# Decay attention: the future cleared by a GpSimd select, the value products and their chain one slot later, six weight buffers

## The reference

```python
Q, K, V = proj(Wq, bq), proj(Wk, bk), proj(Wv, bv)      # 16 heads of 8
scores = einsum('bhid,bhjd->bhij', Q, K) / sqrt(8)
delta = ti[:, None] - ti[None, :]                       # query minus key position
scores = where(delta < 0, -inf, scores) + where(delta < 0, 0, -abs(delta))
out = einsum('bhij,bhjd->bhid', softmax(scores), V) @ Wo.T + bo
```

## Time and profile before

| | |
|---|---|
| median of 3 runs | 1361.05 us (1360.64 to 1365.32) |
| profiled execution | span 1358.3 us; its own device time is not listed, so what lies around the span is taken from the median: 2.7 us |
| instructions | 25046 |
| busy share of the span | PE 79%, DVE 65%, ACT 50%, POOL 41%, PEld 52% |
| second pass of the decay attention | first product at 737.7 us, last at 900.2 us |
| PE, 820 to 860 us | 37.82 of 40 us busy, TensorE's granted clock 1.00 |

### The profile page before, as it was taken

One profiled execution on the slowest core, in us unless ns is written; L12 is line 12 of the kernel. 1 busy time (PEld: TensorE's weight loads), 2 busy tenths in 40 slices (PEclk: granted clock), 3 DMA queues, 4 the chain that ended last, 5 costly groups with the idle time before them and its releaser, 6 DMA issues. The chain is left out here.

```text
span 1358.3 us, 25046 instructions
## 1 busy us (share of the span) xinstructions
PE 1079.5 (79%) x8292; PEld 708.4 (52%) x8292; DVE 881.0 (65%) x2989; ACT 685.8 (50%) x1268; POOL 559.6 (41%) x740
## 2 busy tenths in 40 slices
PE   8877777778189553299936999969977999899998
PEld 3222232336188553299934777744434777654544
DVE  6799999976455456377549888843648878840201
ACT  4786656644044301133206888737856888541221
POOL 4489988853633314544426444100025555100000
PEclk9799999998599765599978999989997999999999
DMA  2997000002422206211120000020612000000000
GB/s 63 206 202 126 0 1 0 1 0 71 140 61 57 92 7 219 70 41 44 37 74 1 2 3 3 2 53 6 203 47 89 3 2 3 2 1 0 16 0 16
DMA packets 85742, 66.77 MB, mean 49 GB/s; under 512 B 15102, under 2 KB 70412, under 8 KB 85612
## 3 DMA queue, kind: packets, MB, share of 16 engines
q1 hardware_dynamic: 79916, 53.65, 17.3%
q0 software_dynamic: 4544, 9.38, 1.9%
q10 hardware_dynamic: 1152, 2.10, 0.4%
HBM read 36.52 MB, written 28.59 MB: 48 GB/s over the span
## 5 line engine op out<-in xcount | busy, mean ns | idle before, releaser
L1076 POOL TENSOR_TENSOR hC<-h,Cs 128x1024 f32<-128x1024 f32 x64 | 150.8, 2356 | 35.3 <-DVE h L973 34.7
L786 PE MATMUL bank<-hC,ident 128*128 128x512 f32 x256 | 128.1, 624 | 45.1 <-POOL hC L1076 43.0
L973 DVE TENSOR_TENSOR_SCAN h<-bank,state,dBx 128x512 f32<-128x512 f32 x128 | 157.3, 1271 | 2.2
L1457 POOL DMA_INDIRECT moe_answers<-moe_yw,moe_xg x78 | 83.7, 1073 | 128.9 <-DVE moe_yw L1634 70.9
L2608 DVE CUSTOM_DVE_ANT_0 decay_below<-bank,decay_q_mask 128x256 bf16<-128x256 f32 x256 | 97.3, 419 | 23.3 <-PE bank L2420 22.4
L786 PEld LDWEIGHTS bank<-hC,ident 128*128 128x128 f32 x256 | 44.9, 192 | 103.9 <-POOL hC L1076 67.1
L2608 DVE CUSTOM_DVE_ANT_0 window_below<-bank,window_q_mask 128x192 bf16<-128x192 f32 x256 | 80.3, 353 | 28.6 <-PE bank L2420 27.0
L2548 ACT ACTIVATE decay_pb<-bank 128x512 f32<-128x512 f32 x128 | 76.2, 598 | 33.5 <-PE bank L2435 32.6
L885 ACT ACTIVATE bank<-dt,A 128x512 f32<-128x512 f32 x128 | 83.2, 683 | 18.7 <-DVE h L973 17.4
L1528 PE MATMUL bank<-moe_xgT,moe_wac 128*128 128x128 f32 x624 | 86.4, 284 | 6.5 <-issue 4.0
L1543 PE MATMUL bank<-moe_wd,moe_hT 128*128 x624 | 83.2, 278 | 5.7 <-DVE moe_hT L1621 2.5
(11 more groups left out here) (482 smaller groups left out, 2797.2 us busy)
## 6 DMA issues: line engine op xcount, KB each, us to landing
moe_slots<-blank SPq DMA_DIRECT2D x16, 1040.0 KB, 16.9
deep_rows<-token_weights SPq DMA_DIRECT2D x32, 256.0 KB, 3.9
moe_xg<-moe_slots SPq DMA_DIRECT2D x78, 65.0 KB, 1.9
moe_wa<-in_moe_w SPq DMA_DIRECT2D x2, 2048.0 KB, 9.7
moe_back<-moe_answers SPq DMA_DIRECT2D x8, 256.0 KB, 5.3
moe_back<-moe_answers ACTq DMA_DIRECT2D x8, 256.0 KB, 6.0
moe_wu<-in_moe_wu SPq DMA_DIRECT2D x1, 2048.0 KB, 15.4
deep_w<-in_deep_w SPq DMA_DIRECT2D x3, 512.0 KB, 6.5
```

The costliest lines, as they stand in the source:

```text
L786: last = nc.tensor.matmul(sum_bank(hh)[:], k.ident[:], hC[:, u % 2, hh, :], start=(n == 0), stop=(n == NS - 1))
L973: v.tensor_tensor_scan(h[:, u % 2, hh, :], decay_bank(u, hh)[:], dBx[:, u % 2, hh, :], state[:, n, hh:hh + 1], ALU.mult, ALU.add).then_inc ...
L1076: g.tensor_tensor(hC[:, u % 2], h[:, u % 2], Cs[:, u % 2, None, :].to_broadcast([P, H, CW]), ALU.mult).then_inc(q_hC, 1)
L1457: nc.gpsimd.indirect_dma_start(answers, bass.IndirectOffsetOnAxis(index, 0), yw[:, i % NY, :], None)\
```

## The change

For `windowed=False` only:

- the second pass has no mask product; its first product opens the bank. So that a future key's exponential stays finite, slot 7 of `qp` and `kp`, zero until now, gets constants that lower the scores of keys in a later block of 32 by 2P
- GpSimd sets the weights of future keys to zero after the exponential, one `affine_select` of 2 x 128 columns in place for each slot; the value products wait for that (`s_low`) and not for the exponential
- `pb` has six buffers in place of four
- value products in slots 4, 6, 0 and 2 in place of 3, 5, 7 and 1, and each step of the chain behind them one slot later; `longest` goes from slot 6 to slot 2
- POOL's list is now by slots: a select in each, `split` for y+4 ahead of the select of slot 2, `lengths` for y+4 ahead of that of slot 4, X0 at the end of tile 0

```diff
@@ zeros
+                for j in range(1, 4):
+                    e.memset(self.qp[i][0:32 * j, :, C + 1, 3 * i + j - 1], 1.0)
+                    e.memset(self.kp[i][32 * max(j, 2):P, :, C + 1, 3 * i + j - 1], -2.0 * P)
+                e.memset(self.kp[i][32:64, :, C + 1, 3 * i], -2.0 * P)
@@ masks
-        yield from mask(self.k_mask, -1, ((BW, P), (P, 0)))
-        if not windowed:
+        if windowed:
+            yield from mask(self.k_mask, -1, ((BW, P), (P, 0)))
+        else:
@@ softmax_mixer
+        more = None if windowed else k.sb(name + "_pb_more", [P, 2, 2 * HW], F32, only_here)
+        SLOTS_P = 4 if windowed else 6
+        later = 0 if windowed else 1
@@ second_pass
-            masked(out)
+            if windowed:
+                masked(out)
...
-                                            q2[:, y % 2, g, 0:b - a], start=False, stop=(j == 1 and s == 1),
-                                            skip_group_check=True)
+                                            q2[:, y % 2, g, 0:b - a], start=(not windowed and j == 0 and s == 0),
+                                            stop=(j == 1 and s == 1), skip_group_check=True)
@@ values
-            pe.wait_ge(s_ex, y * G + 2 * m + 2)
+            pe.wait_ge(s_ex if windowed else s_low, y * G + 2 * m + 2)
@@ tensor
-                    if w == 0 and inside(y - 2):
+                    if w == later and inside(y - 2):
                         project(pe, y - 2)
                     if w == 1 and inside(y + 3):
                         turn_k(pe, y + 3)
-                    if w == 1 and inside(y - 1):
+                    if later and w == 0 and inside(y - 1):
+                        values(pe, y - 1, 2)
+                    if w == 1 + later and inside(y - 1):
                         values(pe, y - 1, 3)
                     if w == 3 and inside(y + 5):
                         qkv(pe, y + 5)
-                    if w in (3, 5, 7) and inside(y):
+                    if w in ((4, 6) if later else (3, 5, 7)) and inside(y):
                         values(pe, y, (w - 3) // 2)
-                    if w == 4 and inside(y - 1):
+                    if w == 4 + later and inside(y - 1):
                         to_queries(pe, y - 1)
                     if w == 5 and inside(y + 1):
                         turn_maxima(pe, y + 1)
-                    if w == 6 and inside(y - 1):
+                    if w == 6 + later and inside(y - 1):
                         to_features(pe, y - 1)
@@ weights, scalar
-            wait(act, s_pv, (n - 4) // 2 + 1)
+            wait(act, s_pv, (n - SLOTS_P) // 2 + 1)
...
-                    if w == 2 and inside(y - 1) and not windowed:
+                    if w == 3 and inside(y - 1) and not windowed:
                         copy_values(act, y - 1)
@@ vector, in the order of a slot: maximum, split_maxima, then
+                    if later and w == 0 and inside(y - 2):
+                        take_features(dve, y - 2)
-                    if w == 1 and inside(y - 2):
+                    if w == 1 + later and inside(y - 2):
                         add(dve, y - 2)
...
+                    if not windowed and w == 2 and inside(y + 3):
+                        longest(dve, y + 3)
-                    if w == 5 and inside(y - 1):
+                    if w == 5 + later and inside(y - 1):
                         normalise(dve, y - 1)
                     if w == 6 and inside(y + 1):
                         maxima_onto_q(dve, y + 1)
-                    if w == 6 and not windowed and inside(y + 3):
-                        longest(dve, y + 3)
-                    if w == 7 and inside(y - 1):
+                    if w == 7 and not later and inside(y - 1):
                         take_features(dve, y - 1)
+        def clear_future(pool, y, w):
+            pool.wait_ge(s_ex, y * G + w + 1)
+            own_keys = kept_weights(y * G + w).rearrange("p (j q) -> p j q", j=2)[:, :, BW:HW]
+            nc.gpsimd.affine_select(out=own_keys, in_=own_keys, compare_op=ALU.is_ge, fill=0.0, base=0,
+                                    pattern=[[0, 2], [1, P]], channel_multiplier=-1).then_inc(s_low, 1)
@@ gpsimd
+                for y in range(T):
+                    for w in range(G):
+                        if w == 2 and inside(y + 4):
+                            split(pool, nc.gpsimd, y + 4)
+                        if w == 4 and inside(y + 4):
+                            lengths(pool, y + 4)
+                        clear_future(pool, y, w)
+                    if y == 0:
+                        nc.gpsimd.tensor_tensor(X0[:], ...)
```

More of the change, by code:

```diff
@@ L2166, in __init__ @@
         self.q_mask = sb("q_mask", [P, self.HW], BF16)
-        self.k_mask = sb("k_mask", [P, 2, self.MW], BF16)
+        self.k_mask = sb("k_mask", [P, 2, self.MW], BF16) if windowed else None
         self.place = None if windowed else sb("place", [P, 2])
@@ L2232, in zeros @@
                 e.memset(self.kp[i][:, :, C, 7 - i], -float(P))
+                yield
+                for j in range(1, 4):
+                    e.memset(self.qp[i][0:32 * j, :, C + 1, 3 * i + j - 1], 1.0)
+                    e.memset(self.kp[i][32 * max(j, 2):P, :, C + 1, 3 * i + j - 1], -2.0 * P)
+                e.memset(self.kp[i][32:64, :, C + 1, 3 * i], -2.0 * P)
+                yield
             last = e.memset(self.qp[i][:, :, C, 3], 1.0)
@@ L2291, in columns @@
                 yield
-    MASKS = {True: 16, False: 15}
+    MASKS = {True: 16, False: 12}
     def ready(self, engine):
@@ L2343, in softmax_mixer @@
         s_longest = sem("longest")
+        s_low = None if windowed else sem("future_cleared")
         s_rot_v, s_rot_p, s_sp_v, s_sp_p = (sem(n) for n in ("rot_vector", "rot_pool", "split_vector", "split_pool"))
@@ L2367, in softmax_mixer, with kept_weights @@
         below = k.sb(name + "_below", [P, HEADS, HW], BF16, only_here)
+        more = None if windowed else k.sb(name + "_pb_more", [P, 2, 2 * HW], F32, only_here)
+        SLOTS_P = 4 if windowed else 6
+        later = 0 if windowed else 1
+        def kept_weights(n):
+            slot = n % SLOTS_P
+            return pb[:, slot, :] if slot < 4 else more[:, slot - 4, :]
         qkv_bank = lambda y: bank[2 + y] if y < EARLY else bank[6]
@@ L2450, in values @@
                                             V[:, (y - 1 + s) % RV, 4 * m + u, :],
-                                            pb[:, g % 4, j * HW + a:j * HW + b],
+                                            kept_weights(y * G + g)[:, j * HW + a:j * HW + b],
                                             start=(s == 1), stop=(s == 0), skip_group_check=True)
@@ L2545, in weights @@
             n = y * G + w
-            wait(act, s_pv, (n - 4) // 2 + 1)
+            wait(act, s_pv, (n - SLOTS_P) // 2 + 1)
             act.wait_ge(s_t, n + 1)
-            nc.scalar.activation(pb[:, w % 4, :], bank[2 + w % 2][:, 0:2 * HW], ACT.Exp).then_inc(s_ex, 1)
+            nc.scalar.activation(kept_weights(n), bank[2 + w % 2][:, 0:2 * HW], ACT.Exp).then_inc(s_ex, 1)
         def copy_values(act, y):
@@ L2766, in gpsimd @@
             m.ready(pool)
-            if not windowed:
-                lengths(pool, 0)
[L2769 to L2780, removed]
+            if windowed:
+                for y in range(OWN, T):
+                    rotate(pool, nc.gpsimd, y)
+                    split(pool, nc.gpsimd, y)
+            else:
+                lengths(pool, 0)
+                split(pool, nc.gpsimd, OWN)
+                lengths(pool, 1)
+                split(pool, nc.gpsimd, OWN + 1)
+                lengths(pool, 2)
+                lengths(pool, 3)
+                for y in range(T):
[6 more added lines that the diff above has]
+                    if y == 0:
+                        nc.gpsimd.tensor_tensor(X0[:], k.X[:], bo[:, None, :].to_broadcast([P, T, P]), ALU.add)\
+                            .then_inc(s_x0, 1)
         yield Engines(sync, gpsimd, tensor, scalar, vector), vector_head
```

## The result

The changed kernel takes 1376.21 us (median of 4 runs, 1373.51 to 1378.58) against 1362.38 (4 runs, 1360.64 to 1365.32) for the kernel before: a ratio of 1.0094, 95% interval 1.0073 to 1.0114 (the quotient of the two medians is 1.0102, inside it). It is slower, on the side that was forecast and by more: 1368.8 was predicted, 1376.2 came, inside the range by 0.8. The profiled span went from 1358.3 to 1371.8, +13.5 where the sum had +7.7.

What follows compares the result with a forecast made beforehand. A closed loop of waits across PE, ACT and DVE was taken to set the 10.56 us period. Terms +7.7 (eleven tiles), +1 (start), -1 (end) gave +7.7 on 1361.05, so 1368.8 us; range 1354 to 1377.

Steps and rivals of the forecast that it cites:

- A: Forecast case: the loop through take_features, copy_values and normalise lengthens tiles by 0.55 to 1.1 us; 1364 to 1374, 55%.
- rival C: Selects hold DVE's cast and subtraction on the loop, 0.7 us a tile more, or POOL sets the period; 1377, 10%.
- The period: Time from one tile's projection to the next: from 10.56 to 11.26 us, 0.70 longer.
- the walk: One tile of the new order, followed step by step from slot 0's first product to the next tile at 11.26 us.
- Eleven tiles, +7.7: Tiles 2 to 12, where the longer loop binds, each 0.70 us longer: 7.7 us in all.
- Between 0 and +2, taken +1: Stage start: X0 moved to tile 1, selects and split queue behind it, values of slots 4 and 6 wait; +1 us.
- The end: Tiles 13 to 15: PE rules and loses masks, but the last select precedes the last values; -2 to 0, taken -1.
- The masks, the constants and the six buffers at nothing: Setup memsets on DVE, less POOL mask work, and six buffers: memsets 0 to +1, taken 0; buffers cost nothing.
- The 2.7 us around the span: The median time lay 2.7 us above the profiled span of 1358.3, and this was carried over to the forecast.
- Rival B: PE's stream stays the bound and the moved steps find room; 1354, or 1347 if all eight masks come off; 20%.
- Rival D: The loop is shorter by some of the pitches and cancels with the masks; 1357 to 1364, 15%.
- What would show it: Signs: projections 11.1 to 11.4 us apart, weights idle 0.5, turn_maxima idle about 1, PE under 90%, 128 selects of 0.4.

Runs made afterwards that it cites:

- the last two of the table: Changed kernel with three moves taken back, X0 in pieces, longest in slot 6 ahead of tile 0: 1350.03 us; the same plus kT's second half first: 1342.65 us.

## Why the prediction was right, and where it was short

- **The case.** A was the likeliest and its mechanism is what happened; its 1364 to 1374 did not hold the time, for the head and X0 below and for 2.1 us behind the stage. That the whole range held it, by 0.8, is luck: its upper end was rival C's time, and C's mechanism did not happen.
- **The period.** Mechanism and size held: 11.15 against 11.26, +0.59 against +0.70 a tile. The three steps it was put down to (take_features behind split_maxima, copy_values ahead of kT, normalise ahead of the sum onto q) were taken back one by one and gave 0.63, 0.36 and 0.47, and together their sum. Of the walk's 0.11 too much, 0.08 lies between projection's weights and the second half of kT.
- **Eleven tiles, +7.7.** They gave +6.7, of which 0.34 is the one tile of 11.49 that X0 made, and that goes with X0.
- **The start of the stage: the term that was mis-sized.** "Between 0 and +2, taken +1" had only X0 in it, which cost 3.4 up to the projection of tile 2, and 3.8 with the odd tile of 11.49. The way it was to cost (selects queued behind X0, values waiting for them) is not what the trace shows: PE's one long wait there, 2.96, was for the row maxima that stood behind DVE's held subtraction, and from the start of X0 at 752.90 to 763 PE waited for no select. The sum had the hold move from tile 0 to tile 1 as if that changed nothing. In the kernel before, the hold of 3.5 us costs PE a wait of 1.32 us:

```profile
746.61 0.62 PE L2403 MATMUL bank<-identb,decay_mp 128*128 128x128 bf16 x8 [1.32 <-DVE decay_mp L2649]
```

From the first second-pass product to the projection of tile 2 that kernel still takes 22.89 us, and the changed one with X0 in pieces, without any hold, 22.85; so the hold seems to have been nearly free where it was, though no run takes it out of the kernel before. And the move of `longest` from slot 6 to slot 2 had no term at all, though its condition can be read from the code: it waits for `lengths`, and ahead of tile 0 that runs late. The head grew by 2.8: the wait of 2.01 and the low clock behind it, and an early rise of the clock that no run ties to the change (pairs alike in that give 1.2, or 3.0 and more). Together the head and X0 took 6.2 where the sum had 1.
- **The end.** -1 forecast, -2.2 came. From the projection of tile 13 to the last it takes 28.10 us before, 25.92 after, 26.15 with only the mask product off and 25.76 after without selects: the products make nearly all of it, and the selects cost 0.2 at most.
- **The masks, the constants and the six buffers at nothing.** No run sets these apart; the entry moved by 0.6, within its scatter.
- **The 2.7 us around the span.** In every timed run on record the time lies 1.6 to 1.8 above the span, so about 1 us of this term was scatter between runs.
- **Rival B** (PE's stream stays the bound) fell as written: the masks bring 0.41 a tile alone, but the moves took more. By its own test it fell too: DVE reached take_features at 1.75 and not by 1.2, and turn_maxima still waited 0.84 for kT.
- **Rival C** gave the right time, 1377, for the wrong reason. Casts of L2658 took 0.28 in the steady tiles, not 0.6; the select was 0.41, and from 770 to 890 no weights of value products idled more than 0.2 us for one. The run without selects shows the hold it described, from `split`, worth 0.4 a tile (11.46 against 11.06). The Trainium skill, "SBUF - State Buffer", section "Who interferes with whom", has it that a VectorE instruction with two SBUF inputs contends with one on GpSimd that reads SBUF, and that the engine that issues first keeps the shared ports for its whole instruction while the other blocks; by that rule the trace agrees (4.43 us beside 4.52, and 0.33 beside 0.42).
- **Rival D** (the loop shorter, cancels with the masks) fell: 11.15.
- **What would show it.** Projections 11.15 apart (11.1 to 11.4 forecast), weights idle 0.64 (0.5 or more), turn_maxima idle 0.84 (about 1), PE 88% (under 90), 128 selects of 0.41. All five as put.

## What to carry to other kernels

When work is taken off the busiest engine of a hand-ordered pipeline, find the loop of waits that sets its period before moving anything: steps moved "a slot later" cost what they now stand in front of, and here three of them (0.63, 0.47 and 0.36 us) outweighed the removed products (0.41 on the old loop). Order within a slot decides as much as the slot: a copy ahead of an exponential that must wait anyway, normalise behind the maximum that waits, take_features ahead of the small steps of split_maxima, were together worth 1.45 us a tile without any change of work. And look at the filling of the pipeline apart from its middle: a step moved earlier can wait there for a helper engine that is late only there, and here a one-off of 4.5 us on GpSimd was better cut in pieces. Compare two traces of such a part only after their granted clocks ahead of it.

## What the runs showed of the hardware that was not expected

- Taking instructions off GpSimd can make VectorE slower: without the selects `split` slid beside VectorE's two small steps, and the tile went from 11.15 to 11.46 us. What counts is where GpSimd's instructions lie, not how many there are.
- VectorE's row maxima are not held by GpSimd: with one input in PSUM and one in SBUF, the maximum of 843.99 begins inside a select (843.67 to 844.08) and takes 0.42; all 256 of the changed kernel take 0.409 to 0.426 us, as in the kernel before. In the kernel without selects the whole X0 sum (748.0 to 752.5) has maxima beside it, and they take 0.41 to 0.43.
- A wait of 2 us on TensorE in the filling of the pipeline was followed by a granted clock of 0.52 from 730 to 735 us. From 5 to 10 us behind the first row maximum the clock is 0.50 to 0.75 in all eight kernels with that order and 1.00 in the six others. The seven of the eight without the mask product took 17.6 to 17.9 us for the head, so this repeats.
- The same code can meet a different clock: ahead of the head it was 0.50 for ten us in some kernels and 0.6 to 0.7 in others with the same order of work up to there (0.50 in the last two of the table, 0.69 and 0.65 with `longest` in slot 6 ahead of tile 0), and the heads without the wait took 14.6 to 14.9 or 16.3 to 16.4 us accordingly.
